# A four-layer transformer kernel: second layer's output and down products as float32r products of split operands

## The reference, cut to what matters

```python
qkv = xn @ w_qkv                       # 16 heads of 64
attn = softmax(q @ k.T / 8 + mask)     # causal, and near or among the first 64
attention = (attn @ v) @ w_out         # 1024 x 128

scores = sigmoid(xn @ gate_w.T)        # 8 experts, the best two of them
for e, wu, wd in experts:
    w_t = sum(where(sel == e, top_scores, 0))
    h = square(relu((xn * w_t) @ wu.T))   # 256 wide
    out += h @ wd.T
```

## Time and profile before

| | us |
|---|---|
| median of three runs | 2044.68 (2041.1 to 2047.77) |
| the profiled execution | 2037.25 |
| its span, first to last instruction | 2035.4 |
| TensorE busy | 1858.2 (91% of the span) |
| VectorE busy | 1358.9 (67%) |
| ScalarE busy | 1129.1 (55%) |
| GpSimd busy | 872.4 (43%) |

### The profile page before, as it was taken

The page is one execution under the profiler, slowest core; times in us unless marked ns, Lnnn a source line. Parts: engine busy times, 40 slices in busy tenths (PEclk is TensorE's granted clock), DMA queues, the critical chain, the costliest instruction groups (busy, mean ns, idle before and its releaser), DMA issues.

```text
span 2035.4 us, 39644 instructions
## 1 busy us (share of the span) xinstructions
PE 1858.2 (91%) x13018; PEld 1310.2 (64%) x13018; DVE 1358.9 (67%) x4809; ACT 1129.1 (55%) x3366; POOL 872.4 (43%) x1361
## 2 busy tenths in 40 slices
PE   5788888479999999999999899999998999999998
PEld 2555555256666666666766566666666777777776
DVE  6999983266666566665665666666664777777775
ACT  3445253155555555555544455555555877777785
POOL 3111355635555555555555311112113555555554
PEclk9889699789999999999999999999998999999999
DMA  6100015650110201101010000000000000000000
GB/s 192 29 1 1 2 29 126 139 164 11 32 43 1 43 1 43 29 16 43 1 43 1 1 1 1 1 1 1 1 1 1 2 7 7 7 7 7 7 2 12
DMA packets 74969, 53.60 MB, mean 26 GB/s; under 512 B 7056, under 2 KB 72976, under 8 KB 73872
## 3 DMA queue, kind: packets, MB, share of 16 engines
q1 hardware_dynamic: 69136, 46.73, 8.0%
q0 software_dynamic: 5632, 4.33, 1.6%
HBM read 40.30 MB, written 10.75 MB: 25 GB/s over the span
## 4 chain that ended last, share of the span: by engine, by line
PE 63%; DVE 11%; ACT 4%; issue 3%; POOL 1%; DMA 0%; POOLq 0%; DVEq 0%; ACTq 0%
PE bank L1305 5%; PE bank L2187 4%; PE bank L1280 4%; PE bank L2174 3%; PE bank L1267 3%; PE bank L2162 3%; PE bank L1288 2%; PE bank L1255 2%; PE bank L2159 2%; PE bank L1252 2%; PE bank L1679 2%; PE bank L1750 2%; PE bank L2139 1%; PE bank L2140 1%; PE bank L2141 1%
## 5 line engine op out<-in xcount | busy, mean ns | idle before, releaser
L1553 POOL TENSOR_TENSOR work<-work 128x128 f32<-128x128 f32 (+1 forms) x512 | 243.1, 506 | 239.5 <-DVE work L1483 239.5
L2397 POOL TENSOR_TENSOR work<-work 128x128 f32<-128x128 f32 (+1 forms) x512 | 243.4, 506 | 224.3 <-DVE work L2331 224.2
L1559 POOL TENSOR_TENSOR work<-work 128x512 f32<-128x512 f32 x128 | 135.7, 1060 | 87.6 <-PE bank L1305 69.9
L1488 DVE COPY work<-bank 128x384 f32<-128x384 f32 x256 | 133.8, 547 | 31.3 <-PE bank L1280 31.3
L1381 ACT ACTIVATE work<-bank 128x512 f32<-128x512 f32 x64 | 38.2, 597 | 199.6 <-PE bank L1243 199.6
L1496 DVE SCALAR_TENSOR_TENSOR work<-bank,w_f 128x512 f32<-128x512 f32 x96 | 66.3, 691 | 120.5 <-PE bank L1299 120.5
L1360 ACT ACTIVATE work<-work 128x128 f32<-128x128 f32 x256 | 100.6, 393 | 83.0 <-DVE work L1479 83.0
L2336 DVE COPY work<-bank 128x384 f32<-128x384 f32 x256 | 134.1, 545 | 17.7 <-PE bank L2187 17.4
L2242 ACT ACTIVATE work<-work 128x128 f32<-128x128 f32 x256 | 100.5, 392 | 60.2 <-DVE work L2327 60.2
L2243 ACT ACTIVATE work<-work 128x256 f32<-128x256 f32 x256 | 126.9, 496 | 0.0
L1361 ACT ACTIVATE work<-work 128x256 f32<-128x256 f32 x256 | 126.8, 495 | 0.0
(11 more groups left out here) (399 smaller groups left out, 5450.3 us busy)
## 6 DMA issues: line engine op xcount, KB each, us to landing
w_f<-gates SPq DMA_DIRECT2D x48, 256.0 KB, 6.1
w_const<-gates SPq DMA_DIRECT2D x16, 256.0 KB, 5.8
w_l<-in_l SPq DMA_DIRECT2D x1, 3210.5 KB, 15.3
w_l<-in_l SPq DMA_DIRECT2D x2, 1540.0 KB, 7.7
w_f<-in_f SPq DMA_DIRECT2D x1, 3072.0 KB, 14.1
x_sb<-in_x SPq DMA_DIRECT2D x4, 512.0 KB, 5.7
normed_rows<-work SPq DMA_DIRECT2D x1, 2048.0 KB, 9.3
even_experts<-x_sb SPq DMA_DIRECT2D x8, 256.0 KB, 3.6
```

The source lines that it names most:

```text
L1488: dve.tensor_copy(pt[u], PS[u][:, 0:384]).then_inc(s_te.s, 1)
L1553: ins_ = pool.tensor_tensor(w, w, spread(rc[:, g % 2, u, q:q + 1], w.shape[1]), ALU.mult)
L1559: pool.tensor_tensor(h2[u % 2], hs[u % 2], hs[u % 2], ALU.mult).then_inc(f_q.s, 1)
L2397: ins_ = pool.tensor_tensor(w, w, spread(rc[:, g % 2, u, q:q + 1], w.shape[1]), ALU.mult)
```

## The change

The output and down products of the second layer become three float32r products each. For the output ScalarE writes `ot_hi` (as before, now rounded) and VectorE `ot_lo` (`heads_rest`, after the second of the four `turned_out`). For the down product ScalarE squares the gated tile into `h2_hi` (`squares_hi`), GpSimd squares it too, in float32 (`sq`), and subtracts the one from the other into `h2_lo`. Both weights are split once: ScalarE writes `wout_hi` and `down_hi` in iteration -1, behind a wait for the first layer's last sums (`x_sum`), and VectorE the rests in iteration 1. The room for this is found by a ring of four gate tiles in place of eight, by `yT` at the end of `x_sb`, and by two loads that come later: the third layer's weights (before: after the gate tiles of pass 0; now: before those of pass 1) and the last layer's query and key weights (before: with the masks in layer 0; now: after the last down product). `gates(i)` moves ahead of the iteration's first `gated`.

```diff
-            gate = [late_f0(4, 128) for _ in range(6)] + [C[n].rearrange("p (t k) -> p t k", k=128) for n in ("tri", "vsel")]
+            GATES = 4
+            gate = [late_f0(4, 128) for _ in range(GATES)]
...
@@ output(g), TensorE
-                    past(pe, s_ot, g + 1)
-                    pe.matmul(ACC[:, :], L["wout"][:, j * 128:(j + 1) * 128], ot[g % 2], start=(j == 0), stop=False,
-                              skip_group_check=True).then_inc(o_f.s, 1)
+                    if g == 0:
+                        past(pe, w_lo, 1)
+                    past(pe, s_or, g + 1)
+                    ws = slice(j * 128, (j + 1) * 128)
+                    pe.matmul(ACC[:, :], wout_hi[:, ws], ot_hi[g % 2], start=(j == 0), stop=False, skip_group_check=True)
+                    pe.matmul(ACC[:, :], wout_hi[:, ws], ot_lo[g % 2], start=False, stop=False, skip_group_check=True)
+                    pe.matmul(ACC[:, :], wout_lo[:, ws], ot_hi[g % 2], start=False, stop=False, skip_group_check=True).then_inc(o_f.s, 1)
@@ down(g), TensorE
-                    past(pe, f_q, 2 * g + 2)
...
+                        past(pe, f_lo, 2 * g + c + 1)
+                        ws = slice((2 * e + c) * D, (2 * e + c + 1) * D)
+                        pe.matmul(ACC[:, :], down_hi[:, ws], h2_hi[c], start=False, stop=False, skip_group_check=True)
+                        pe.matmul(ACC[:, :], down_hi[:, ws], h2_lo[c], start=False, stop=False, skip_group_check=True)
+                        mm = pe.matmul(ACC[:, :], down_lo[:, ws], h2_hi[c], start=False, stop=(e == PAIRS - 1 and c == 1), skip_group_check=True)
@@ ScalarE
+                def squares_hi(u):
+                    past(act, f_h, u + 1)
+                    past(act, f_d, u // 2)
+                    act.activation(h2_hi[u % 2], hs[u % 2], ACT.Square).then_inc(f_hi.s, 1)
...
+                    if 0 <= s - 2 < N:
+                        squares_hi(2 * (s - 2))
                     if s + 1 < N:
                         values_out(s + 1)
+                    if s == -1:
+                        act.wait_ge(x_sum, len(ACC_TILES))
+                        act.activation(wout_hi, L["wout"], ACT.Copy).then_inc(w_hi.s, 1)
+                        act.activation(down_hi, L["down"], ACT.Copy).then_inc(w_hi.s, 1)
+                    if 0 <= s - 2 < N:
+                        squares_hi(2 * (s - 2) + 1)
@@ VectorE
+                def heads_rest(g):
+                    past(dve, s_ot, g + 1)
+                    past(dve, o_f, g - 1)
+                    dve.tensor_tensor(ot_lo[g % 2], HEADS_OUT[:, :], ot_hi[g % 2].bitcast(F32), ALU.subtract).then_inc(s_or.s, 1)
...
+                    if s == 1:
+                        past(dve, w_hi, 2)
+                        dve.tensor_tensor(wout_lo, L["wout"], wout_hi.bitcast(F32), ALU.subtract).then_inc(w_lo.s, 1)
+                        dve.tensor_tensor(down_lo, L["down"], down_hi.bitcast(F32), ALU.subtract).then_inc(w_lo.s, 1)
+                    if 0 < i < PASSES and at == 3:
+                        gates(i)
                     if 0 <= s - 2 < N:
                         gated(2 * (s - 2))
...
-                        if at == 3:
-                            gates(i)
@@ squared(u), GpSimd
-                    pool.tensor_tensor(h2[u % 2], hs[u % 2], hs[u % 2], ALU.mult).then_inc(f_q.s, 1)
+                    pool.tensor_tensor(sq[u % 2], hs[u % 2], hs[u % 2], ALU.mult).then_inc(f_q.s, 1)
+                    past(pool, f_q, u + 1)
+                    past(pool, f_hi, u + 1)
+                    pool.tensor_tensor(h2_lo[u % 2], sq[u % 2], h2_hi[u % 2].bitcast(F32), ALU.subtract).then_inc(f_lo.s, 1)
@@ SP
-                    if i == 0:
+                    if i == 1:
                         sp.dma_start(regions["l2"][:, :], ins["l2"]).then_inc(w_in["l2"], 16)
                         sp.dma_start(regions["l3"][:, 0:width("l3")], ins["l3"]).then_inc(w_in["l3"], 16)
+                    for e in range(E1):
+                        past(sp, f_h, 2 * (PAIRS * i + e - GATES) + 2)
```

More of the change, by code:

```diff
@@ L43 @@
 }
-LOADS = (("const",), ("l0",), ("f0",), ("l1",), ("l2", "l3"), ("qk1",), ("qk3", "masks"))
+LOADS = (("const",), ("l0",), ("f0",), ("l1",), ("l2", "l3"), ("qk1",), ("qk3",), ("masks",))
 def width(pack):
@@ L1132, in second_layer @@
             pt = [carve(384) for _ in range(UNITS)]
-            ot = [carve(512) for _ in range(2)]
-            hs, h2 = [carve(512) for _ in range(2)], [carve(512) for _ in range(2)]
-            yT = carve(512)
+            ot_at = top[0]
+            carve(2, 512)
+            ot_hi = [rounded(f"l1_heads_hi_{p}", "work", ot_at + p * 512, 512) for p in range(2)]
+            hs = [carve(512) for _ in range(2)]
+            h2_at = top[0]
+            carve(2, 512)
+            h2_hi = [rounded(f"l1_squares_hi_{c}", "work", h2_at + c * 512, 512) for c in range(2)]
+            sq1_at = top[0]
+            carve(512)
+            yT = x_t[:, TILES * D:TILES * D + 512]
             nmx, sm, rc = carve(2, UNITS, 2), carve(2, UNITS, 2), carve(2, UNITS, 2)
@@ L1140, in second_layer @@
             in_l0, late_f0 = arena(regions["l0"], width("l0")), arena(regions["f0"][:, width("l3"):], width("f0") - width("l3"))
-            cgt, ceq = in_l0(4, E1 * E1), in_l0(4, E1 * E1)
-            gate = [late_f0(4, 128) for _ in range(6)] + [C[n].rearrange("p (t k) -> p t k", k=128) for n in ("tri", "vsel")]
+            GATES = 4
+            gate = [late_f0(4, 128) for _ in range(GATES)]
+            const_at = {n: sum(w for _, w in PACKS["const"][:[m for m, _ in PACKS["const"]].index(n)]) for n in ("tri", "vsel")}
+            ot_lo = [rounded(f"l1_heads_lo_{p}", "w_const", const_at[n], 512) for p, n in enumerate(("tri", "vsel"))]
+            wout_hi, wout_lo = rounded("l1_wout_hi", "w_f0", width("l3") + GATES * 512, WIDE), rounded("l1_wout_lo", "w_l1", WIDE, WIDE)
+            down_hi, down_lo = rounded("l1_down_hi", "qk", 2 * WIDE, E1 * HID1), rounded("l1_down_lo", "w_l1", 2 * WIDE + E1 * HID1, E1 * HID1)
+            h2_lo = [rounded("l1_squares_lo_0", "w_l0", 0, 512), rounded("l1_squares_lo_1", "work", sq1_at, 512)]
+            sq = [in_l0(512), work[:, sq1_at:sq1_at + 512]]
+            cgt, ceq = in_l0(4, E1 * E1), C["tileno"].rearrange("p (t k) -> p t k", k=E1 * E1)
             Q0, Q1 = slice(256, 384), slice(0, 256)
@@ L1187, in second_layer @@
                 ("gated", 2 * N), ("squared", 2 * N), ("down", N), ("sum_out", PASSES), ("gates", PASSES)))
+            f_hi, f_lo, s_or = (Count(sem("l1_" + n), 0, total) for n, total in (("squares_hi", 2 * N), ("squares_lo", 2 * N), ("heads_rest", N)))
+            w_hi, w_lo = Count(sem("l1_out_hi"), 0, 2), Count(sem("l1_out_lo"), 0, 2)
             g_out, g_in = sem("l1_gates_out"), [sem(f"l1_gates_in{p}") for p in range(4)]
@@ L1261, in weighted @@
                     taken(pe, "v", i * PAIRS + j // 4 * 4 + 3)
-                    past(pe, s_ot, g)
+                    past(pe, s_or, g)
                     v, at = v_sb[j // 4], j % 4 * 128
@@ L1302, in down @@
                     e = g % PAIRS
-                    past(pe, f_q, 2 * g + 2)
+                    if g == 0:
+                        past(pe, w_lo, 2)
                     for c in range(2):
-                        mm = pe.matmul(ACC[:, :], L["down"][:, (2 * e + c) * D:(2 * e + c + 1) * D], h2[c], start=False, stop=(e == PAIRS - 1 and c == 1),
-                                       skip_group_check=True)
+                        past(pe, f_lo, 2 * g + c + 1)
[3 more added lines that the diff above has]
+                        mm = pe.matmul(ACC[:, :], down_lo[:, ws], h2_hi[c], start=False, stop=(e == PAIRS - 1 and c == 1), skip_group_check=True)
                     mm.then_inc(f_d.s, 1)
@@ L1517, in dve_ @@
                     if 0 <= s - 2 < N:
-                        for u in (1, 2, 3):
+                        turned_out(s - 2, 1)
+                    if 0 <= s - 3 < N:
+                        heads_rest(s - 3)
+                    if 0 <= s - 2 < N:
+                        for u in (2, 3):
                             turned_out(s - 2, u)
@@ L1580, in sp_ @@
                     sp.wait_ge(g_out, 16 * (i + 1))
-                    for e in range(E1):
-                        past(sp, f_h, 2 * (PAIRS * (i - 1) + e) + 2)
-                        sp.dma_start(gate[e], gates_d[i % 2].rearrange("(t e) k -> e t k", e=E1)[e].unsqueeze(0).to_broadcast([128, 4, 128])).then_inc(g_in[e // 2], 16)
-                    if i == 0:
+                    if i == 1:
                         sp.dma_start(regions["l2"][:, :], ins["l2"]).then_inc(w_in["l2"], 16)
                         sp.dma_start(regions["l3"][:, 0:width("l3")], ins["l3"]).then_inc(w_in["l3"], 16)
+                    for e in range(E1):
+                        past(sp, f_h, 2 * (PAIRS * i + e - GATES) + 2)
```

(3 more changed lines are left out.)

8 lines of the change are left out of this document (4 added, 4 removed).

## The result

The changed kernel takes 2017.38 us (median of 4 runs, 2014.67 to 2019.06) against 2042.89 us (2039.95 to 2047.77) for the kernel before in the same measurement: ratio 0.9871, 95% interval 0.9848 to 0.9893. Measured again later the ratio was 0.9885 (0.9870 to 0.9901). The gain is 25.5 us in the first measurement, where 23.0 were forecast. The profiled execution has a span of 2015.5 us.

The account below looks back on a forecast made before the run. The prediction took TensorE's list of work to bound the second layer. 2037.25 - 31.4 + 0.8 + 0 + 3.4 + 2.2 + 2 = 2014.3, that is -23.0; from the 2044.7 median, 2022 us, 8-in-10 range 2009 to 2036.

Parts of the forecast that it names:

- The products: Second layer's output and down products: three float32r products each save 0.49 us per step, -31.4 us over 64 steps.
- GpSimd: Its added squares and subtractions fit each step, 8.2 to 9.5 of 10.0 us: cost 0.
- ScalarE and VectorE per step: ScalarE's two added squares and VectorE's added subtraction stay under 7.3 of 10.0 us per step: cost 0.
- The gates moved: End of each pass: a 1.5 us stall before the values replaces 1.48 at the maxima: 0, bounds -7 and +8.
- the lock bites in all of the gates: Rival, chance 0.04: GpSimd delays all nine VectorE gate operations, stall 4.7 us plus clock loss, +36 us, giving 2058.
- The start: Layer's start: ScalarE's weight splits +3.4 us, VectorE's subtractions +2.2, possible half clock +2.
- can halve the clock: Layer's start: an idle gap of TensorE can halve its clock, +2 us, bounds 0 and 5.
- The last step: Layer's end: VectorE's subtraction is on the path only in the last step, which nothing else fills: +0.8 us.
- The loads: Third layer's weights load in pass 1, last layer's after the last down product, both in time: 0, at worst 2 us.
- The other rivals: Gates' stall halves the clock, 2044 (0.12); GpSimd becomes the bound, 2060 (0.03); start and loads worse, 2030 to 2036 (0.10).

Follow-up runs that it names:

- products: The changed kernel with the gates put back behind both gated tiles, so only the float32r products remain: 2043.95 us, ratio 1.0018 to the kernel before.
- move: The kernel before with only the gates put ahead of the first gated tile, output and down products still float32: 2029.81 us, ratio 0.9954.

## Why the prediction was right, and where not

The forecast was 2022, -23.0; measured 2017.4, -25.5 (the kernel before was itself 1.8 us faster in this measurement than the median the forecast started from). The layer itself, -24.3 in the profiles, can be split at the gates' stores: six passes of -4.19 make -25.1; the stretch ahead of them, to the second store, went from 90.6 to 93.8 (+3.2), the one behind from 98.5 to 96.1 (-2.4).

- **The products** (-31.4 forecast, 0.49 a step): right. The step went from 10.49 to 10.00, and each split alone gave its share within 0.02. The rule of the Trainium skill that the prediction weighed, "FP8 and Floating Point Precision" (TensorE Precision Notes), four passes for true float32, would have given 0.65 a step; the measured 0.49 decides against using it as a time here.
- **GpSimd** (0): right, with a term mis-sized. The rest took 1.28 us, not 1.13, so the list is 8.4 us per step for a forecast of 8.2 to 9.5. The down products do not come 5 us after the last rest but 3.6 (it ends at 799.48, they start at 803.03). The two runs with more squares show where it would decide: 1.04 us more is free, 2.08 more is not.
- **ScalarE and VectorE per step** (0): right; neither stands in TensorE's waits in an ordinary step.
- **The gates moved** (0; a wait of 1.5 for one of 1.48): right as a sum, 1.36 for 1.48, and 0.26 less per pass in all. But the prediction treated the move as a thing of its own that brings nothing, and the runs show that it carries the change. Left where they were, the gates would have met the new rests on GpSimd; the wait is then 3.41, the clock halves, and the products' 3.9 us per pass shrink to 0.56. The prediction came out right all the same because the place it took as given was the better one. The step that failed is the comparison with the old wait as it was, where the right one is with the wait that the old place would have had under the new load.
- **The rival "the lock bites in all of the gates"**: its mechanism is real and its price near (4.7 us of wait plus 2 of clock forecast, 3.4 plus up to 2.7 measured), but in the place that the change gives up. Where the gates are now, only GpSimd's weight groups run beside them, and the third to fifth operation lose 0.4, 0.1 and 0.3 us in the case shown. The Trainium skill's rule in "SBUF — State Buffer" (SBUF: two separate sides) says that a GpSimd operation and a VectorE operation with two SBUF inputs, or in a two-port mode, shut each other out for a whole instruction. The traces agree: an operation ends within 0.04 to 0.3 us of a GpSimd operation's end, and is at its own length when GpSimd's work is taken away. That the first gate operation, with one input, is held too (1239 ns for 169) fits the second half of the rule; that it runs in such a mode no trace shows.
- **The start** (+3.4 +2.2 +2): +3.2 with five steps' savings of 2.5 inside, so +5.7 for 7.6. Both waits came: ScalarE's splits ahead of the first copies, and 2.31 us for VectorE's rests. But this is one execution. In the second profile of the same kernel the stretch lasts 95.4 us, so the start costs 7.3, near the forecast. The granted clock over the layer's first 35 us was 0.85 before, 0.77 in the first profile and 0.70 in the second. Behind the same wait of 2.31 us it stayed at 1.00 in the first, and read 0.50 in the second (TensorE's timeline and the windows there):

```profile
442.22 1.43 PE L1295 MATMUL bank<-w_const,work 128*128 128x128 f32 x6 [2.31 <-DVE work L1515]
```

```profile
444.00:446.00 2.00, 2.00 (x10) 1.70 (x8) 1.13 (x4) 1.89 (x8) 1.62 (x4) 0.50 0.00 0
```

So the forecast's "can halve the clock", with bounds of 0 and 5 us, was the right form. How much of the start is the clock and how much the splits wasn't separated; moving the splits gives 3.7 to 5.3 back.

- **The last step** (+0.8): mis-sized. The stretch behind the last store holds eleven steps' savings, 5.4, and is only 2.4 shorter: +3.0. TensorE waits not once but in the last three iterations for the heads' rest (3.0 us in all), since without query and key products it reaches the output early. With the down split alone, where there is no such rest, the stretch is 95.5 although its steps are 0.17 longer.
- **The loads** (0): right. SP issued them at 512.85 and 513.24, they landed 10.8 and 13.6 us later, and no gated tile waited for a transfer.
- The other rivals did not occur. The clock reads 1.00 behind the wait of 1.36.

-31.4 + 5.7 + 3.0 - 6 x 0.26 = -24.3, the layer's difference. In this profile the forecast's start was too dear by 1.9 and its end too cheap by 2.2; these two errors cancel, so the sum is better than its terms, and that is luck. In the second profile the sum is -31.4 + 7.3 + 3.0 - 6 x 0.26 = -22.7 (the layer: -22.8), with the start as forecast and only the end mis-sized. The later measurement of the whole kernel gave a gain of 24.2 us.

## What to carry to other kernels

When a change loads an engine, look at what the other engine does beside the new work, and place its short dependent chains where the loaded engine is idle or waits. Here the same nine small operations cost TensorE 1.4 or 5.0 us per pass (6 in the worst one) by their place alone, and in the kernel's time that difference was as large as the gain of the whole change. Judge the parts of a change in combination: "products" and "move" alone gave -0.56 and -1.59 per pass, together -4.19. And a helper engine's added work is free in the steady steps as long as its list stays under the bounding engine's; two runs with dummy work show on which side of that edge a kernel is.

## What was not expected of the hardware

- A one-input operation of VectorE on 128x32 elements took 1239 ns beside GpSimd's rest, 169 to 171 without it. The rest of the normalized input, two inputs, went from a mean of 681 ns before to 1617 in the changed kernel (1749 but for the first, which has no squares beside it).
- The price of a TensorE wait is not its length. After the waits of 1.36 us per pass the granted clock stayed at 1.00 every time. The wait of 2.31 us at the layer's start, which seven profiles have, was followed by 1.00 in three of them and by 0.50 in four, and the two profiles of the changed kernel itself differ in this: so whether such a wait costs the clock is not to be read from one execution. After each of the seven of 3.41 us it read 0.50, for 2.7 to 5.8 us. A wait at the maxima goes with a pass about 0.65 us longer than one of the same length ahead of the values; 0.17 of that was found, the rest not.
- GpSimd's subtraction with a float32r result took 1.28 us for 128x512, where a quarter of the third layer's 128x2048 is 1.13.
